# Score matmuls as row tiles of 32 partitions, and the causal mask of the second pass as a selection on GpSimd

## The chip, the cores and the metric

The kernel runs on one core of one Trainium2 chip, in one launch. The metric is the device time of one execution in microseconds. A core has TensorE (matmuls, into PSUM), VectorE, ScalarE, GpSimd and SyncE (DMA issue). Each works through its own list in order, and they wait for each other on semaphores.

## The reference

The input is x of 4 batches x 1024 tokens x 128 channels. Two blocks follow; each is a residual around layer normalisations.

```python
# block 1: causal attention with ALiBi, 16 heads of 8 channels
scores = einsum('bhqd,bhkd->bhqk', q, k) * 8 ** -0.5 + slope[h] * (i - j)
scores = where(tril, scores, -inf)
x = x + layernorm(softmax(scores) @ v @ Wo + bo)
# block 2, on layernorm(x): attention without a mask, then a mixture of 8 experts
y = y + layernorm(attention(y)); y = y + layernorm(moe(y))
out = x + layernorm(y)
```

Both attentions run over all 1024 tokens with 16 heads of 8 channels.

## The kernel before

The program is a row pass, a first attention (`at1`, causal, about 48 to 740 us), a second row pass, a second attention (`at2`, no mask, about 803 to 1726 us), and a tail with the experts. Both attentions are the function `attention` with another `Plan`.

Heads are taken in groups of four; a group of one batch is a slot `s`, 16 in all. A head has 32 of the 128 partitions: its 8 channels three times over (high and low parts of a split, for precision in fp32r) and rows for the ALiBi term and the maximum. For each slot there are two passes over the scores:

- pass `a` (line 333): queries on the output partitions, keys along the columns. VectorE takes the maximum of each row (line 466). In the causal plan keys beyond the query tile are left out, and the diagonal block of 128 x 128 gets -1e30 by a second matmul (line 337). Chunks with 128 or 256 keys are packed, four or two heads to one matmul of 512 columns: 38 chunks per slot, 22 of them with a mask. The second attention has 64 of 512 columns.
- pass `b` (line 360): keys on the partitions, queries along the columns, with the negated maximum of the query in the contraction (`fqm`). In the causal plan eight of twelve blocks have a diagonal, masked by another matmul (line 363). ScalarE takes the exponential (line 415) into `probs`. The `pv` step (line 378) multiplies them by the values and by a column of ones: four matmuls per block, each head to its own 32 output partitions (the profile shows eight instructions).

Score matmuls contract over all 128 partitions: the keys are kept in four copies, `km`, each with the rows of the other heads set to zero. `proj` (lines 201 to 203 and 316) projects queries or keys of half a sequence into the bank `misc`. ScalarE copies it to `u` (line 404), and the split follows: `hi`, `part`, then `fq` for queries, or `fk` and the masked write of `km` (2048 elements per partition, line 569) for keys. The first slot's split is VectorE's (lines 442 to 454); all others are GpSimd's (lines 556 to 569), three slots ahead of use.

The order is written out in `Plan.body` and followed by every engine. A slot is a list of steps, one per block (12 causal, 16 otherwise). Step i holds, in this order: the four `b` matmuls of block i+2, interleaved with three to five `a` chunks of the next slot; `m` (the maxima are finished on VectorE, line 474); `proj`; `otr` and `mtr` (four turning matmuls each); `pv` of block i+1; `oev` (PV is copied out). In the causal plan `proj` is at steps 1, 2, 5, 6. The scores have three banks per pass, PV one, and projections and turns share `misc`. The prologue does the projections of slots 0 to 2 and pass `a` of slot 0. The last three slots have no `proj`, and the last one no `a`.

## Time and profile before

| | us |
|---|---|
| median of 3 runs | 2288.22 |
| lowest, highest | 2284.65, 2291.63 |
| span of the profiled execution | 2287.5 |
| TensorE busy | 2102.9 |
| VectorE busy | 1671.8 |
| ScalarE busy | 1373.5 |
| GpSimd busy | 977.3 |

The span runs from the first to the last instruction of the profiled execution. The profile gives no time for that execution beside its span; the median of the runs is 0.7 us longer. Busy time is the union of the instructions of an engine. Ends of matmuls are modelled, so successive matmuls overlap in the timeline; the distance between their starts is what tells the pace. The granted clock (PEclk) is TensorE's as a share of full speed.

### The profile page before, as it was taken

How to read it: one execution, taken by the hardware profiler on the slowest of the kernel's cores; microseconds unless marked ns; L12 is line 12 of the kernel's file. 1: busy time of each engine (PE TensorE's matmuls, PEld its weight loads, DVE VectorE, ACT ScalarE, POOL GpSimd, SP SyncE). 2: the span in 40 equal slices, each digit the busy share in tenths (PEclk: the TensorE clock that was granted, in tenths of full speed). 3: DMA queues.
4: the chain of work that ended last, by engine and by line, in shares of the span. 5: the costliest groups of instructions: out<-in, count | busy, mean ns of one | idle time of the engine just before them, and what ended most of it. 6: DMA issues, size and time to landing. Idle time of an engine off the chain costs nothing. (4 is left out here: it accounts for less than half of the span.)

```text
span 2287.5 us, 41083 instructions
## 1 busy us (share of the span) xinstructions
PE 2102.9 (92%) x11100; PEld 1223.1 (53%) x11100; DVE 1671.8 (73%) x3157; ACT 1373.5 (60%) x2647; POOL 977.3 (43%) x744
## 2 busy tenths in 40 slices
PE   5899999999999679999999999999993999999996
PEld 4455555555554534555555555555531666666664
DVE  5766667666672787777777777778822899998986
ACT  4266566666666616666666666666672655555654
POOL 3665464553610355333333333342002466565554
PEclk7799999999999679999999999999996999999998
DMA  2000000000000300000000000000001100000000
GB/s 59 1 2 1 3 1 1 2 2 1 1 1 2 110 0 1 2 1 1 2 1 1 2 1 1 1 1 1 1 1 61 51 19 19 2 19 19 19 10 10
DMA packets 27508, 24.96 MB, mean 11 GB/s; under 512 B 2409, under 2 KB 21110, under 8 KB 27282
## 3 DMA queue, kind: packets, MB, share of 16 engines
q1 hardware_dynamic: 26400, 21.91, 3.2%
q8 instruction: 103, 1.69, 0.3%
q14 instruction: 123, 1.01, 0.2%
q10 hardware_dynamic: 882, 0.36, 0.1%
HBM read 13.87 MB, written 6.29 MB: 9 GB/s over the span
## 5 line engine op out<-in xcount | busy, mean ns | idle before, releaser
L466 DVE TENSOR_REDUCE at_mx<-at_a 128x1 f32<-128x512 f32 (+3 forms) x1632 | 1010.8, 675 | 358.7 <-PE at_a L333 249.5
L415 ACT ACTIVATE at_probs<-at_b 128x512 f32<-128x512 f32 (+3 forms) x1792 | 888.6, 558 | 474.0 <-PE at_b L360 292.7
L333 PE MATMUL at_a<-at_km,at_fq 128*128 128x512 f32 (+1 forms) x1632 | 704.8, 439 | 20.4 <-DVE at_mx L466 9.8
L360 PE MATMUL at_b<-at_fqm,at_km 128*128 128x512 f32 (+3 forms) x1792 | 710.8, 404 | 11.4 <-ACT at_probs L415 7.6
L333 PEld LDWEIGHTS at_a<-at_km,at_fq 128*128 128x128 f32 x1632 | 316.3, 194 | 290.0 <-DVE at_mx L466 224.4
L360 PEld LDWEIGHTS at_b<-at_fqm,at_km 128*128 128x128 f32 x1792 | 339.8, 191 | 205.5 <-ACT at_probs L415 120.3
L378 PE MATMUL at_pv<-at_probs,at_vst 128*32 128x512 f32 (+3 forms) x3584 | 437.9, 561 | 1.5 <-ACT at_probs L415 1.5
L556 POOL TENSOR_TENSOR at_hi<-at_u,split_sign 128x512 fp32r<-128x512 f32 x120 | 124.9, 1041 | 441.1 <-ACT at_u L404 306.5
L1172 ACT ACTIVATE t_hid<-t_bank_h,b1t 128x512 f32<-128x512 f32 x256 | 174.3, 689 | 195.9 <-DVE t_hid_lo L1306 113.1
L1306 DVE TENSOR_TENSOR t_hid_lo<-t_hid,t_hid_hi 128x512 fp32r<-128x512 f32 x256 | 225.6, 917 | 15.0 <-ACT t_hid_hi L1179 11.8
L569 POOL TENSOR_TENSOR at_km<-at_fk,head_mask 128x2048 fp32r<-128x2048 f32 x60 | 216.1, 3602 | 11.2 <-POOL at_fk L567 11.0
L1340 POOL TENSOR_TENSOR t_hid_hi<-t_hid,pow_cols 128x512 fp32r<-128x512 f32 x112 | 141.1, 1275 | 129.6 <-ACT t_hid L1172 129.0
L404 ACT ACTIVATE at_u<-at_misc,bias 128x512 f32<-128x512 f32 x128 | 88.2, 689 | 124.7 <-PE at_misc L203 58.0
L526 POOL COPY at_vst<-tokens 128x256 f32 (+1 forms) x32 | 13.0, 405 | 328.5 <-PE at_pv L378 328.2
L201 PE MATMUL t_bank_y<-t_hid_hi,t_w2hi 128*128 128x512 f32 x256 | 106.6, 416 | 31.3 <-DVE t_weighed L1315 26.8
L559 POOL TENSOR_TENSOR at_part<-at_hi,split_sign 128x512 f32<-128x512 f32 x120 | 125.0, 1042 | 21.4 <-POOL at_hi L556 21.4
L378 PEld LDWEIGHTS at_pv<-at_probs,at_vst 128*32 128x32 f32 x3584 | 70.6, 108 | 117.1 <-ACT at_probs L415 85.1
L363 PE MATMUL at_b<-ident,causal_mask 128*128 128x128 bf16 x512 | 117.8, 232 | 0.0
L203 PE MATMUL t_bank_y<-t_hid_hi,t_w2lo 128*128 128x512 f32 x256 | 102.2, 399 | 0.0
L202 PE MATMUL t_bank_y<-t_hid_lo,t_w2hi 128*128 128x512 f32 x256 | 101.9, 398 | 0.0
L337 PE MATMUL at_a<-causal_mask,ident 128*128 128x128 bf16 (+2 forms) x352 | 91.7, 260 | 0.0
L564 POOL TENSOR_TENSOR at_fq<-at_part,at_u 128x512 fp32r<-128x512 f32 x60 | 77.0, 1284 | 10.7 <-POOL at_part L559 10.7
(211 smaller groups left out, 2410.3 us busy)
## 6 DMA issues: line engine op xcount, KB each, us to landing
t_raw<-L_ffn_W SPq DMA_DIRECT2D x16, 256.0 KB, 3.1
x_first<-L_attn_x SPq DMA_DIRECT2D x4, 512.0 KB, 7.3
second_x_in<-L_attn_x SPq DMA_DIRECT2D x8, 256.0 KB, 3.1
kept<-second_joined SPq DMA_DIRECT2D x8, 256.0 KB, 2.6
kept_u<-second_normed SPq DMA_DIRECT2D x8, 256.0 KB, 2.0
t_heads_in<-tokens SPq DMA_DIRECT2D x8, 256.0 KB, 2.6
t_u_in<-kept_u SPq DMA_DIRECT2D x8, 256.0 KB, 3.1
t_x_in<-kept SPq DMA_DIRECT2D x8, 256.0 KB, 3.1
```

Of the source, the lines that this page charges most:

```text
L333: mm = pe.matmul(scores, fq[g][:, qt * P:(qt + 1) * P], km[g][:, heads[0]:heads[0] + k, kh * HALF:kh * HALF + w], start=True, stop=not dia ...
L360: mm = pe.matmul(out[:, 0:w], km[g][:, j, kt * P:(kt + 1) * P], fqm[g % 2][:, q0:q0 + w], start=True, stop=not diagonal)
L363: mm = pe.matmul(out[:, 0:P], causal_mask[:, :], ident16[:, :], start=False, stop=True)
L378: mm = pe.matmul(pv_bank[HW * j:HW * (j + 1), HALF - w:HALF], vst[g % 2][:, kt, j, :], probs[(n % 2) * GH + j][:, 0:w], start=(kt == 0), s ...
L415: act.activation(probs[(t % 2) * GH + j][:, 0:w], b_bank[n % 3][:, 0:w], ACT.Exp).then_inc(exp_done, 1)
L466: dve.tensor_reduce(mx[:, kh, qt, heads[0]:heads[0] + k], a_bank[n % 3][:, 0:k * w].rearrange("p (k w) -> p k w", k=k), AX.X, ALU.max).the ...
L556: pool.tensor_tensor(hi[:, :], un[:, :], split_sign[:, 2:3].broadcast_to([P, HALF]), ALU.add).then_inc(pool_step, 1)
L559: pool.tensor_tensor(part[:, :], hi[:, :].bitcast(F32), split_sign[:, m:m + 1].broadcast_to([P, HALF]), ALU.mult).then_inc(pool_step, 1)
L569: pool.tensor_tensor(km[g][:, :, half], fk[:, None, :].broadcast_to([P, GH, HALF]), head_mask[:, :, None].broadcast_to([P, GH, HALF]), ALU ...
L1172: act.activation(hid[:, f, :], h_bank[f][:, :], ACT.Gelu, bias=b1t[:, f, e:e + 1]).then_inc(hidden["act"], 1)
L1306: dve.tensor_tensor(hid_lo[e % 2][:, f, :], hid[:, f, :], hid_hi[e % 2][:, f, :].bitcast(F32), ALU.subtract).then_inc(hidden["dve"], 1)
L1340: pool.tensor_tensor(out, a, b, op).then_inc(stage["pool"], 1)
```

## The change

- `km` goes. Score matmuls of both passes take the 32 partitions of one head from `fk` and `fq` or `fqm`, so that they are row tiles of 32 x 128. GpSimd and VectorE no longer write the masked copies; a key split ends with `fk`.
- Each chunk of pass `a` has one head. The causal plan now has 48 chunks per slot, 32 with a mask, and the mask matmul stays a full 128 x 128. `a_next`, the share of the next slot's chunks in the last four steps, becomes 16 of 48.
- The heads of a block of pass `b` are taken in the order 2, 3, 0, 1 (`b_head`).
- Pass `b` has no mask matmul. The exponentials of a block lie together in one `probs` tile, and for the eight diagonal blocks GpSimd runs an `affine_select` over 4 x 128 elements per partition that puts zero where the key is later than the query. `pv` of such a block waits for it (`masked`). GpSimd meets it in its list where `pv` stands.

```diff
-                per = max(1, HALF // n)
-                per = 4 if per >= 4 else per
-                for j in range(0, GH, per):
-                    self.chunks.append((qt, kh, list(range(j, j + per)), n))
+                for j in range(GH):
+                    self.chunks.append((qt, kh, j, n))
...
+        self.diagonals = [t for t, (qh, kt) in enumerate(self.quads) if causal and kt * P >= qh * HALF]
...
+def b_head(n):
+    return (n + 2) % GH
...
-        km = [sb(f"km{i}", [P, GH, T], F32R) for i in range(4)]
+        fk = [sb(f"fk{i}", [P, T], F32R) for i in range(4)]
...
-        probs = [sb(f"probs{i}", [P, HALF]) for i in range(8)]
+        probs = [sb(f"probs{i}", [P, GH, HALF]) for i in range(2)]
...
-                        mm = pe.matmul(scores, fq[g][:, qt * P:(qt + 1) * P],
-                                       km[g][:, heads[0]:heads[0] + k, kh * HALF:kh * HALF + w],
+                        rows = slice(HW * j, HW * (j + 1))
+                        mm = pe.matmul(scores, fq[g][rows, qt * P:(qt + 1) * P],
+                                       fk[g][rows, kh * HALF:kh * HALF + w],
                                        start=True, stop=not diagonal)
                         if diagonal:
-                            mm = pe.matmul(scores[:, :, w - P:w], ident16[:, :],
-                                           causal_mask[:, None, :].broadcast_to([P, k, P]),
+                            mm = pe.matmul(scores[:, w - P:w], ident16[:, :], causal_mask[:, :],
                                            start=False, stop=True)
...
-                        mm = pe.matmul(out[:, 0:w], km[g][:, j, kt * P:(kt + 1) * P],
-                                       fqm[g % 2][:, q0:q0 + w], start=True, stop=not diagonal)
-                        if diagonal:
-                            mm = pe.matmul(out[:, 0:P], causal_mask[:, :], ident16[:, :],
-                                           start=False, stop=True)
+                        rows = slice(HW * j, HW * (j + 1))
+                        mm = pe.matmul(out[:, 0:w], fk[g][rows, kt * P:(kt + 1) * P],
+                                       fqm[g % 2][rows, q0:q0 + w], start=True, stop=True)
...
                         done(pe, exp_done, NB, s, GH * n + GH - 1)
+                        if n in plan.diagonals:
+                            done(pe, masked, len(plan.diagonals), s, plan.diagonals.index(n))
...
                 for what, ds, n in steps:
                     s = s0 + ds
+                    if what == "pv" and n in plan.diagonals:
+                        await_(exp_done, NB, s, GH * n + GH - 1)
+                        block_ = probs[n % 2][:, :, 0:P]
+                        pool.affine_select(block_, block_, [[0, GH], [1, P]], ALU.is_ge, 0.0, base=0,
+                                           channel_multiplier=-1).then_inc(masked, 1)
                     if what != "proj":
                         continue
...
-                    if m == 0:
-                        pool.tensor_tensor(fq[g][:, half], part[:, :], un[:, :],
-                                           ALU.add).then_inc(split_done, 1)
-                    else:
-                        pool.tensor_tensor(fk[:, :], part[:, :], un[:, :], ALU.add).then_inc(pool_step, 1)
-                        await_(pool_step, count, s, step + 2)
-                        pool.tensor_tensor(km[g][:, :, half],
-                                           fk[:, None, :].broadcast_to([P, GH, HALF]),
-                                           head_mask[:, :, None].broadcast_to([P, GH, HALF]),
-                                           ALU.mult).then_inc(split_done, 1)
+                    dst = fk if m else fq
+                    pool.tensor_tensor(dst[g][:, half], part[:, :], un[:, :], ALU.add).then_inc(split_done, 1)
```

## Rows read from the trace of the kernel before

**Rows 1.** The page's first part: busy us (share of the span) xinstructions, whole run.
```profile
PE 2102.9 (92%) x11100; PEld 1223.1 (53%) x11100; DVE 1671.8 (73%) x3157; ACT 1373.5 (60%) x2647; POOL 977.3 (43%) x744
```

**Rows 2.** Windows of the two attentions; columns: length, five engines' busy us, PEclk, DMA.
```profile
120.00:700.00 580.00, 576.14 (x3761) 308.73 (x3760) 390.45 (x684) 363.34 (x764) 272.27 (x194) 0.99 0.01 2
900.00:1600.00 700.00, 693.30 (x3637) 374.54 (x3636) 545.36 (x951) 477.26 (x895) 262.56 (x188) 1.00 0.01 1
```

**Rows 3.** Starts of the step m (line 474), first and second attention.
```profile
L474 DVE TENSOR_TENSOR at_mfull<-at_mx x15: 193/381/669, 137.0 to 705.2; 128x32 f32<-128x32 f32 x15
...
L474 DVE TENSOR_TENSOR at_mfull<-at_mx x15: 191/192/194, 915.4 to 1674.9; 128x32 f32<-128x32 f32 x15
```

**Rows 4.** Waits in the second attention: us in total, times, longest.
```profile
DVE at_mx L466 <- PE at_a L333: 145.9, 195, 3.1
```

**Rows 5.** Timeline of TensorE, second attention: start us, us, then the instruction.
```profile
1209.11 1.07 PE L378 MATMUL at_pv<-at_probs,at_vst 128*32 128x512 f32 x8
...
1211.83 0.40 PE L360 MATMUL at_b<-at_fqm,at_km 128*128 128x512 f32 x1
1212.16 1.06 PE L378 MATMUL at_pv<-at_probs,at_vst 128*32 128x512 f32 x8
1213.16 0.50 PE L333 MATMUL at_a<-at_km,at_fq 128*128 128x512 f32 x1
1213.49 0.39 PE L360 MATMUL at_b<-at_fqm,at_km 128*128 128x512 f32 x1
1213.72 0.40 PE L333 MATMUL at_a<-at_km,at_fq 128*128 128x512 f32 x1
```

**Rows 6.** Timeline, second attention: VectorE in a full step, ScalarE in the last slot.
```profile
892.58 2.48 DVE L466 TENSOR_REDUCE at_mx<-at_a 128x1 f32<-128x512 f32 x4 [0.55 <-PE at_a L333]
...
1714.06 2.07 ACT L415 ACTIVATE at_probs<-at_b 128x512 f32<-128x512 f32 x4 [0.55 <-PE at_b L360]
```

**Rows 7.** Groups of GpSimd by form, first attention: busy us, mean ns, idle before.
```profile
L569 POOL TENSOR_TENSOR at_km<-at_fk,head_mask 128x2048 fp32r<-128x2048 f32 x26 | 93.6, 3602 | 4.6 <-POOL at_fk L567 4.5 <-ACT at_u L404 0.2
L556 POOL TENSOR_TENSOR at_hi<-at_u,split_sign 128x512 fp32r<-128x512 f32 x51 | 53.1, 1041 | 150.1 <-PE at_b L360 124.8 <-ACT at_u L404 20.7 <-POOL at_km L569 4.6
L526 POOL COPY at_vst<-tokens 128x256 f32<-128x256 f32 x3 | 1.2, 400 | 48.4 <-PE at_pv L378 48.4
```

**Rows 8.** Timeline of VectorE in the prologue of the second attention.
```profile
807.81 2.29 DVE L454 TENSOR_TENSOR at_km<-at_fk,head_mask 128x2048 fp32r<-128x2048 f32 x1
```

**Rows 9.** Groups of line 466 by form, first attention.
```profile
L466 DVE TENSOR_REDUCE at_mx<-at_a 128x1 f32<-128x512 f32 x342 | 220.5, 687 | 115.4 <-PE at_a L333 74.2 <-PE at_a L337 40.8
L466 DVE TENSOR_REDUCE at_mx<-at_a 128x1 f32<-128x384 f32 x116 | 64.4, 558 | 42.3 <-PE at_a L337 39.1
```

**Rows 10.** Timeline of TensorE, first attention: two scores around a masking matmul.
```profile
404.44 0.40 PE L333 MATMUL at_a<-at_km,at_fq 128*128 128x512 f32 x1
...
405.03 0.40 PE L333 MATMUL at_a<-at_km,at_fq 128*128 128x512 f32 x1
```

**Rows 11.** Timeline, first attention, a projection step: TensorE, ScalarE, then GpSimd.
```profile
403.53 0.64 PE L378 MATMUL at_pv<-at_probs,at_vst 128*32 128x256 f32 x8
...
403.72 0.69 ACT L404 ACTIVATE at_u<-at_misc,bias 128x512 f32<-128x512 f32 x1 [0.92 <-PE at_misc L316]
...
404.75 1.04 POOL L556 TENSOR_TENSOR at_hi<-at_u,split_sign 128x512 fp32r<-128x512 f32 x1 [9.86 <-PE at_b L360]
...
407.19 1.29 POOL L567 TENSOR_TENSOR at_fk<-at_part,at_u 128x512 f32<-128x512 f32 x1 [0.18 <-POOL at_part L559]
408.66 3.60 POOL L569 TENSOR_TENSOR at_km<-at_fk,head_mask 128x2048 fp32r<-128x2048 f32 x1 [0.18 <-POOL at_fk L567]
```

**Rows 12.** TensorE after an idle stretch: timeline row, then windows (columns as rows 2).
```profile
860.52 0.63 PE L346 MATMUL at_misc<-ident,at_mpad 128*128 128x128 f32 x4 [2.64 <-DVE at_mpad L481]
...
862.00:865.00 3.00, 2.90 (x8) 2.00 (x9) 1.92 (x4) 0.00 (x0) 2.82 (x2) 0.50 0.01 3
865.00:868.00 3.00, 2.71 (x8) 1.14 (x6) 3.00 (x6) 1.01 (x2) 2.72 (x2) 0.93 0.00 0
```

More of the change, by code:

```diff
@@ L261, in attention @@
         o_done = sem("o_done")
+        masked = sem("masked")
         init = sem("init")
@@ L319, in emit @@
                     elif what == "a":
-                        qt, kh, heads, w = plan.chunks[n]
+                        qt, kh, j, w = plan.chunks[n]
                         _, g = where(b0, g0, ds)
@@ L327, in emit @@
                         done(pe, a_read, NA, s - back, k)
[L328 removed]
+                        scores = a_bank[n % 3][:, 0:w]
                         diagonal = causal and kh * HALF + w == (qt + 1) * P
[L331 to L334 removed]
+                        rows = slice(HW * j, HW * (j + 1))
+                        mm = pe.matmul(scores, fq[g][rows, qt * P:(qt + 1) * P],
+                                       fk[g][rows, kh * HALF:kh * HALF + w],
                                        start=True, stop=not diagonal)
                         if diagonal:
[L337 to L338 removed]
+                            mm = pe.matmul(scores[:, w - P:w], ident16[:, :], causal_mask[:, :],
                                            start=False, stop=True)
@@ L357, in emit @@
                         w = (qh + 1) * HALF - q0
-                        diagonal = causal and kt * P >= qh * HALF
                         out = b_bank[n % 3]
-                        mm = pe.matmul(out[:, 0:w], km[g][:, j, kt * P:(kt + 1) * P],
-                                       fqm[g % 2][:, q0:q0 + w], start=True, stop=not diagonal)
-                        if diagonal:
-                            mm = pe.matmul(out[:, 0:P], causal_mask[:, :], ident16[:, :],
-                                           start=False, stop=True)
+                        rows = slice(HW * j, HW * (j + 1))
+                        mm = pe.matmul(out[:, 0:w], fk[g][rows, kt * P:(kt + 1) * P],
+                                       fqm[g % 2][rows, q0:q0 + w], start=True, stop=True)
                         mm.then_inc(b_made, 1)
@@ L438, in emit @@
                         un = u[n % 2]
-                        own = 5 * h if m else 5 * h + 3
+                        own = 4 * h + 2 * (n % 2)
                         done(dve, proj_read, 4, s, n)
@@ L447, in emit @@
                         dve.wait_ge(dve_step, own + 2)
-                        if m == 0:
-                            dve.tensor_tensor(fq[g][:, half], part[:, :], un[:, :],
-                                              ALU.add).then_inc(split_done, 1)
-                        else:
-                            dve.tensor_tensor(fk[:, :], part[:, :], un[:, :], ALU.add).then_inc(dve_step, 1)
-                            dve.wait_ge(dve_step, own + 3)
-                            dve.tensor_tensor(km[g][:, :, half],
-                                              fk[:, None, :].broadcast_to([P, GH, HALF]),
-                                              head_mask[:, :, None].broadcast_to([P, GH, HALF]),
-                                              ALU.mult).then_inc(split_done, 1)
+                        dst = fk if m else fq
+                        dve.tensor_tensor(dst[g][:, half], part[:, :], un[:, :], ALU.add).then_inc(split_done, 1)
                     elif what == "a":
-                        qt, kh, heads, w = plan.chunks[n]
+                        qt, kh, j, w = plan.chunks[n]
                         done(dve, a_made, NA, s, n)
@@ L464, in emit @@
                             done(dve, m_step, 2, s - 1, 0)
[L465 to L467 removed]
+                        dve.tensor_reduce(mx[:, kh, qt, j:j + 1], a_bank[n % 3][:, 0:w],
                                           AX.X, ALU.max).then_inc(a_read, 1)
@@ L504, in _ @@
         def _(pool):
-            for semaphore, per in ((split_done, 4), (v_staged, 1)):
-                pool.sem_inc(semaphore, per)
+            for semaphore, per in ((split_done, 4), (v_staged, 1), (masked, len(plan.diagonals))):
+                if per:
+                    pool.sem_inc(semaphore, per)
             pool.memset(mpad[:, :, :], 0.0).then_inc(init, 1)
@@ L552, in emit @@
                     await_(split_done, 4, s, n - 1)
-                    step = 5 * h if m else 5 * h + 3
+                    step = 4 * h + 2 * (n % 2)
                     half = slice(h * HALF, (h + 1) * HALF)
```

26 lines of the change are left out of this document (7 added, 19 removed).

## The prediction

> **What bounds the kernel now.** I read the busy shares of the page first [rows 1]: TensorE 92%, VectorE 73%, ScalarE 60%, GpSimd 43%. Shares average over stages, so next the windows of the two attention stages [rows 2]. In both TensorE is busy 99% of the time; VectorE is busy 67% of the first (causal) attention and 78% of the second. The step `m` runs once per slot (a slot is one batch and group of four heads), so its first and last start give the period [rows 3]: (705.2 - 137.0)/14 = 40.6 us causal, (1674.9 - 915.4)/14 = 54.25 us non-causal. The waits agree: in the second attention VectorE waited 145.9 us for score matmuls [rows 4]. The timeline shows how full TensorE is: a score matmul of 512 columns starts 0.23 us after the last one, a PV group takes 1.00 us until the next matmul starts, and one step of eight scores and PV takes 3.05 us [rows 5]. The chain of waits covers little of these stages; I use it for nothing.
>
> **Step 1: scores as row tiles.** 96 to 128 score matmuls per slot contract over 32 rows instead of 128. They could only become cheaper by running beside each other: the order a j, b j+2, a j+1, b j+3 puts neighbours on different partitions and banks. No row shows a row tile. The nearest is PV: eight instructions of 512 columns, in four column tiles, take 1.00 us together while a single score takes 0.23 [rows 5]; column tiles do overlap. Bounds for one row-tiled score: 0.23 us (no overlap) and 0.06 (four at once). I take 0.12, their geometric mean, since PV shows overlap in the other direction of the array only.
> The Trainium skill ("TensorE: Matmul & The Clock Gate", Part 3) gives four row tiles of 512 columns a speedup of 3.07; by that the score would be 0.076 us. No run here shows it so far.
>
> Second attention: a step on TensorE becomes 8 x 0.12 + 1.00 + 0.2 = 2.2 us, under VectorE's 2.48 us for four reductions [rows 6]. So VectorE is late next. It is busy 0.779 x 54.25 = 42.3 us per slot; three banks cover 3 x 0.6 = 1.8 us of TensorE being elsewhere, enough for a PV (1.3 us with its changes), not for PV plus projection (2.0) or plus turns (1.85) with 0.4 us until the first score is out. Eight such places lose about 0.55 us each: 46.8 us. Gain 7.45 x 15 = 112 us. The last slot has no reductions; its steps go from ScalarE's 2.07 busy + 0.55 waiting [rows 6] towards 2.2: 5 us. Together **-117** (bounds: 0 without overlap, -176 if VectorE never starves, 11.3 x 15 + 7).
>
> **Step 2: no head-masked key copies.** The masked write of 2048 elements goes from GpSimd (3.60 us, two per slot) and, in each prologue, two of 2.29 us from VectorE [rows 7, 8]. In the loop GpSimd's split is three slots ahead: hidden, worth nothing by itself. In the prologues the first scores wait for VectorE's splits, so about 3 us each: **-6** (0 to -10).
>
> **Step 3: causal chunks one head at a time.** 48 reductions for 38: six packed ones of 512 become eight of 128 and eight of 256. From 687 ns at 512 and 558 at 384 [rows 9] a 128 costs about 0.30 and a 256 about 0.43: 5.8 - 4.1 = +1.7 us, VectorE 27.3 + 1.7 = 29.0 us, still under TensorE. The masking matmuls of the first pass go from 22 to 32 per slot.
>
> **Step 4: masks on TensorE.** A masking matmul today lengthens the stream by 0.12 us: two scores and a mask take 405.03 - 404.44 = 0.59 against 2 x 0.23 [rows 10]. The second pass loses 32 of them, 4 us of 40.6. The first pass keeps its own, now a 128-row matmul between 32-row ones. The trace shows what a change of array shape costs: before each PV the next start comes 0.33 us after a 512-column matmul in place of 0.23 [rows 5], 0.10 more, and the same on the way back. So one masked score with the b score beside it: 0.1 + 0.05 + 0.1 + 0.08 of exposed load + 0.17 of columns = 0.5 us, 32 times = 16. The 32 scores left over: 3.8. Unchanged: PV 11.8 (six groups of 1.00, two each of 0.79, 0.57 and 0.36 by their columns, and 12 x 0.2 for changes [rows 5, 11]), projections 3.6 (14 matmuls of 512 columns at 0.23 to 0.33), turns 2.1 (four sets at 0.63 less 0.1 of overlap [rows 12]). Sum 37.3. The same working for the kernel before gives 8.4 + 3.0 of masks for pass a, 8.6 + 4.0 for pass b, and these 17.5: 41.5 where 40.6 is measured, so I take 36.5 (bounds 32, mask as cheap as today, and 41).
> The rule that speaks against this change is in the skill ("TensorEngine Tiling (Array Packing)", Key Properties): changing the tiling mode drains the engine. The 0.10 us in the rows agrees in kind. By a full drain (0.39 us, the duration of a 512 score) each masked pair would be 0.3 us longer, and the causal slot 9 us longer.
>
> **Step 5: the selection on GpSimd.** This is the step that decides. The selection is issued at `pv` in program order; in the list of a step `proj` stands before `pv`, and GpSimd is in order. TensorE now waits at a diagonal `pv` for `masked`, and everything of the next step is queued behind it. Causal projections are at steps 1, 2, 5, 6, the diagonal PVs at steps 0-2 (blocks 1-3) and 7-11. At steps 1 and 2 the selection is thus behind the split of a projection that TensorE has just made. The links are in [rows 11]: PV could start at 403.53; ScalarE's copy ends at 404.41; the three splitting operations start at 404.75 and end at 408.48; the selection can start at 408.66, where the masked copy does now. With 1.04 us for it and 0.2 for the hand-over PV starts at 409.9: a stall of 6.3 us. At step 2 the projection has no ALiBi matmul, and the same links give 6.3 again. At step 7 TensorE passes PV 7 (1.2 us) and the scores of step 7 (2.1) first: 3 us left. Elsewhere the exponentials are done a step earlier (about 2 us before) and the selection is hidden; if it took over 2 us it would bind there too.
> Duration of the selection, 512 elements per partition: no row has it. Below: a copy of 256 takes 0.40, so 0.8; above: 3.60, the masked write [rows 7]. I take 1.04, the elementwise operation of the same size, the nearest row [rows 7]. At 3.6 each stall grows by 2.6, 13 slots x 7.7 = +100.
> Stalls: 6.3 + 6.3 + 3 = 15.6 us, in the 13 slots that project three ahead.
>
> **Step 6: the clock.** After 2.64 us of idle TensorE was granted 0.50 in the next 3 us and 0.93 in the 3 after it [rows 12]: the lower of its two levels, 1.2 GHz, for some 3.4 us. Three stalls per slot cost up to 1.7 us of warm work each; part hides behind VectorE: 4 us (bounds 0 and 6).
>
> Causal slot: 36.5 + 15.6 + 4 = 56.1, +15.5 x 13 = +202. Two other looped slots at 36.5: -8; the last -4. First attention **+190** (bounds: 32 + 15 + 0 = 47 gives +60; 41 + 16 + 6 = 63 gives +290).
>
> **Sum:** +190 - 117 - 6 = +67 us on the profiled execution with its span of 2287.5 us; what lies outside the span I leave as it is. The span is 0.7 us under the median of 2288.22 (runs 2284.65 to 2291.63), so 2355 us for the median.
>
> **Rivals.**
> A, faster: the second attention falls to VectorE's floor (-150 to -176) and the causal slot is cheap between its stalls, 33 + 15 + 1 = 49 us, +8.4 x 13 - 20 = +90. Total 90 - 160 - 6 = -76: 2212 us. For it: VectorE leaves 22% of the second attention idle and TensorE has slack in the new step. Against it: it needs masked pairs at about 0.35 us, cheaper than the two shape changes in the trace allow. With the second attention as forecast the total crosses zero at a stalled slot of 40.6 + 135/13 = 51 us; from there A decides.
> B, no overlap: row tiles run one after another at 0.23 us because each writes all 128 partitions of PSUM. Second attention unchanged, causal slot 41 + 16 + 4 = 61: +265 - 6. Total 2547 us. Against it: PV's column tiles overlap [rows 5].
> C, the stalls are not there (GpSimd is ahead, or the selection overtakes): causal 36.5, -4.1 x 16 = -66; total -189: 2099 us. Against it: the list's order, and the 3.7 us from 404.75 to 408.48 in [rows 11].
>
> **How the numbers follow.** Forecast 0.56; A 0.22; B 0.17; C 0.05. About 0.3% is what a measurement tells from no change. The forecast's own spread (2260 to 2440) leaves a little under 2295, so slower is 0.51 + 0.17 = 0.69; the band within 0.3% gets 0.04 between A and the forecast; faster 0.27. Range: from A's inner half, 2225, up to 2450, which leaves out C, the low end of A, and B.
>
> **What would show it.** Changed profile: score starts about 0.1 us apart and a period near 47 us in the second attention; VectorE over 88% busy there; in the causal one two idle stretches of TensorE of about 6 us per slot, each ending with a selection on GpSimd, and a granted clock under 0.9 on average; a selection near 1.04 us. I am wrong if score starts stay 0.23 us apart (B), if the idle stretches are missing (C), or if masked pairs cost 0.35 us (A).

## The result and the profile after

The changed kernel took 2908.68 us, median of 4 runs (2898.94 to 2924.59), beside 2286.83 us for the kernel before (4 runs, 2284.65 to 2291.63). The ratio is 1.272, 95% interval 1.267 to 1.277: 27% slower. The forecast was 2355 us in a range of 2225 to 2450. The direction was right, the size far outside the range. A run over 1.5% above the fastest of its kernel is marked slow; without such runs e17's median is 2457.64 us and e19's 2242.6, in place of the 2462.01 and 2260.68 given below.

The profiled execution has a span of 2922.9 us, 635.4 more than before. The page of the kernel after: busy shares, then TensorE's busy tenths and the granted clock in 40 slices.

```profile
PE 2426.0 (83%) x10908; PEld 1131.0 (39%) x10908; DVE 1693.7 (58%) x3313; ACT 1379.3 (47%) x2647; POOL 835.7 (29%) x812
...
PE   5888887888888888997788888888888849999997
...
PEclk6555555555555555556579989979999759999998
```

TensorE's share fell from 92% [rows 1] to 83%, and its granted clock is at the lower of its two levels (1.2 of 2.4 GHz) through nearly all of the first attention. The starts of `m` in the two attentions of the kernel after answer to [rows 3]:

```profile
L465 DVE TENSOR_TENSOR at_mfull<-at_mx x15: 191/273/714, 193.2 to 1302.7; 128x32 f32<-128x32 f32 x15
...
L465 DVE TENSOR_TENSOR at_mfull<-at_mx x15: 192/193/194, 1536.9 to 2285.9; 128x32 f32<-128x32 f32 x15
```

The causal slot is (1302.7 - 193.2)/14 = 79.25 us (before: 40.59) and the non-causal one 53.5 (before: 54.25). The 15 starts span 1109.5 us in place of 568.2: 541 of the 635 us. A further 56 lie ahead of them (193.2 against 137.0) and 21 between the last causal `m` and the first of the second attention. These three are in the main the first attention with its prologue, +618 us where +190 was forecast. The second attention's sixteen starts of `m` (the first at 1477.2, before at 858.5) take 8 us less than before, and what follows its last `m` 24 us more (637.0 against 612.6): +16 us where -117 was forecast. Windows of the two attentions after (columns as in [rows 2]):

```profile
330.00:530.00 200.00, 168.56 (x630) 66.26 (x628) 72.55 (x145) 65.56 (x133) 45.73 (x51) 0.53 0.00 1
...
1480.00:2280.00 800.00, 678.33 (x4161) 255.21 (x4165) 630.92 (x1096) 542.71 (x1025) 182.47 (x173) 0.94 0.01 1
```

**The predicted waits are there.** TensorE's wait at PV in the first attention after, in us, times and longest:

```profile
PE at_pv L379 <- POOL at_probs L536: 165.1, 40, 5.5
```

And one of them in the timeline (start, us, instruction, idle before): the query split ends, the selection starts at once, and PV starts when it is over. A single selection takes 636 ns (the group of 124 in the first attention).

```profile
519.39 1.27 POOL L561 TENSOR_TENSOR at_fq<-at_part,at_u 128x512 fp32r<-128x512 f32 x1 [0.18 <-POOL at_part L556]
...
520.61 1.23 POOL L536 TENSOR_SCALAR_AFFINE_SELECT at_probs<-at_probs 128x512 f32<-128x512 f32 x2
...
521.30 1.05 PE L379 MATMUL at_pv<-at_probs,at_vst 128*32 128x512 f32 x4 [1.32 <-POOL at_probs L536]
```

**A masked pair, at the full clock and at half.** TensorE in the first attention after:

```profile
504.80 0.49 PE L362 MATMUL at_b<-at_fqm,at_fk 32*128 32x512 f32 x1
504.80 0.44 PE L336 MATMUL at_a<-at_fk,at_fq 32*128 32x384 f32 x1
505.22 0.23 PE L340 MATMUL at_a<-causal_mask,ident 128*128 128x128 bf16 x1
505.38 0.49 PE L362 MATMUL at_b<-at_fqm,at_fk 32*128 32x512 f32 x1
...
540.19 0.68 PE L362 MATMUL at_b<-at_fqm,at_fk 32*128 32x384 f32 x1
540.19 0.79 PE L336 MATMUL at_a<-at_fk,at_fq 32*128 32x512 f32 x1
540.91 0.29 PE L340 MATMUL at_a<-causal_mask,ident 128*128 128x128 bf16 x1
541.13 0.68 PE L362 MATMUL at_b<-at_fqm,at_fk 32*128 32x384 f32 x1
```

The two row tiles start together; then the 128-row mask comes 0.42 us after them, and the next pair 0.16 us after the mask: 0.58 us for the pair (0.94 at half clock). For scale: before, two scores and a mask took 0.59 us one after another [rows 10]. The overlap that the row tiles win is given back at the mask. Full clock is rare in this stage: it holds here for some 4 us.

**The second attention** reaches the overlap but not the gain. TensorE after, from one PV to the next, in a step without projection or turns:

```profile
1802.89 1.06 PE L379 MATMUL at_pv<-at_probs,at_vst 128*32 128x512 f32 x8
1803.89 0.50 PE L336 MATMUL at_a<-at_fk,at_fq 32*128 32x512 f32 x1
1803.89 0.51 PE L362 MATMUL at_b<-at_fqm,at_fk 32*128 32x512 f32 x3
1804.23 0.40 PE L336 MATMUL at_a<-at_fk,at_fq 32*128 32x512 f32 x2
1805.17 0.49 PE L336 MATMUL at_a<-at_fk,at_fq 32*128 32x512 f32 x1 [0.54 <-DVE at_mx L458]
...
1805.68 1.06 PE L379 MATMUL at_pv<-at_probs,at_vst 128*32 128x512 f32 x8
```

One PV to the next takes 2.79 us where it took 3.05 [rows 5]. The fourth `a` score waits for VectorE to read a bank. VectorE in turn still waits for scores, 157.1 us of 800 (before 145.9 of 700 [rows 4]), the same fifth of the time: both engines wait, in turn.

### The profile page after: what moved, and what is told of

It is laid out like the page before. It is cut to its first block and busy times, and to the rows that moved or that the text cites. A ratio compares the mean times of both kernels' runs of the same rounds, so it can differ in the third digit from the quotient of the medians.

```text
span 2922.9 us, 41409 instructions
## 1 busy us (share of the span) xinstructions
PE 2426.0 (83%) x10908; PEld 1131.0 (39%) x10908; DVE 1693.7 (58%) x3313; ACT 1379.3 (47%) x2647; POOL 835.7 (29%) x812
## 3 DMA queue, kind: packets, MB, share of 16 engines
q14 instruction: 127, 1.04, 0.1%
## 5 line engine op out<-in xcount | busy, mean ns | idle before, releaser
L458 DVE TENSOR_REDUCE at_mx<-at_a 128x1 f32<-128x512 f32 (+3 forms) x1792 | 1041.4, 629 | 868.6 <-PE at_a L336 432.2
L336 PE MATMUL at_a<-at_fk,at_fq 32*128 32x512 f32 (+3 forms) x1792 | 763.2, 564 | 134.1 <-DVE at_mx L458 124.7
L362 PE MATMUL at_b<-at_fqm,at_fk 32*128 32x512 f32 (+3 forms) x1792 | 732.2, 574 | 45.4 <-ACT at_probs L416 45.4
L379 PE MATMUL at_pv<-at_probs,at_vst 128*32 128x512 f32 (+3 forms) x3584 | 589.2, 741 | 165.4 <-POOL at_probs L536 165.4
L336 PEld LDWEIGHTS at_a<-at_fk,at_fq 32*128 32x128 f32 x1792 | 339.4, 234 | 626.5 <-DVE at_mx L458 461.8
L362 PEld LDWEIGHTS at_b<-at_fqm,at_fk 32*128 32x128 f32 x1792 | 301.8, 230 | 290.1 <-ACT at_probs L416 128.6
L553 POOL TENSOR_TENSOR at_hi<-at_u,split_sign 128x512 fp32r<-128x512 f32 x120 | 124.6, 1038 | 984.5 <-ACT at_u L405 984.1
L536 POOL TENSOR_SCALAR_AFFINE_SELECT at_probs<-at_probs 128x512 f32<-128x512 f32 x128 | 80.7, 636 | 399.9 <-ACT at_probs L416 399.9
L340 PE MATMUL at_a<-causal_mask,ident 128*128 128x128 bf16 x512 | 143.7, 281 | 0.0
L340 PEld LDWEIGHTS at_a<-causal_mask,ident 128*128 128x128 bf16 x512 | 52.2, 102 | 153.9 <-issue 144.1
L206 PE MATMUL at_misc<-turned_hi,w_hi 128*128 (+1 forms) x128 | 86.8, 678 | 12.9 <-PEq L598 8.2
L483 DVE RECIPROCAL at_rec<-at_misc 128x16 f32<-128x16 f32 x64 | 16.4, 256 | 137.3 <-PE at_misc L386 137.0
```

What stands on the lines that cost most here:

```text
L206: pe.matmul(out, a[0], b[0], start=start, stop=False)
L336: mm = pe.matmul(scores, fq[g][rows, qt * P:(qt + 1) * P], fk[g][rows, kh * HALF:kh * HALF + w], start=True, stop=not diagonal)
L340: mm = pe.matmul(scores[:, w - P:w], ident16[:, :], causal_mask[:, :], start=False, stop=True)
L362: mm = pe.matmul(out[:, 0:w], fk[g][rows, kt * P:(kt + 1) * P], fqm[g % 2][rows, q0:q0 + w], start=True, stop=True)
L379: mm = pe.matmul(pv_bank[HW * j:HW * (j + 1), HALF - w:HALF], vst[g % 2][:, kt, j, :], probs[n % 2][:, j, 0:w], start=(kt == 0), stop=(n = ...
L458: dve.tensor_reduce(mx[:, kh, qt, j:j + 1], a_bank[n % 3][:, 0:w], AX.X, ALU.max).then_inc(a_read, 1)
```

## The experiments

All slots below are (last - first start of `m`)/14, and "clock" is the granted one in windows of the first attention, both of the profiled execution. Totals are medians. The diffs are against the kernel named.

**1. The selection issued early: e1.** Against the kernel after: GpSimd selects at the last exponential of a block, ahead of `proj` in its list.

```diff
-                    if what == "pv" and n in plan.diagonals:
-                        await_(exp_done, NB, s, GH * n + GH - 1)
+                    if what == "b" and n % GH == GH - 1 and n // GH in plan.diagonals:
+                        await_(exp_done, NB, s, n)
```

> The changed kernel, but GpSimd runs each selection where the last exponential of its block stands in the list, ahead of that step's projection split. Stall theory (the idle stretches of TensorE behind GpSimd cause both the waiting and the half clock of the first attention): the two 5.5 us waits per slot go, the granted clock there rises from 0.52 to at least 0.95, the slot falls from 80.5 to about 38 us, total near 2250 us. Tile theory (a stream of row tiles broken by full-array masks does not get the full clock back once it is lost, and the loop and the prologue lose it without any stall): only the waits go, 12.7 us per projecting slot and the clock stays near 0.52: slot about 67 us, total about 2740 us.

Measured: 2664.95 us, ratio 1.163 (1.157 to 1.170). Slot 61.85. No wait of TensorE for a selection is left, and TensorE is 97% busy, but the clock stays low. Window of e1:

```profile
330.00:530.00 200.00, 194.00 (x796) 79.16 (x796) 90.44 (x182) 82.71 (x170) 58.76 (x65) 0.59 0.01 1
```

The waits and what hangs on them are worth 17.4 us of a slot, of which the waits themselves were 12.7; 21 us over the slot before remain without them. Neither theory's clock or total came out (0.95 and 2250, 0.52 and 2740), but the clock that stays low without a wait is the tile theory's.

**2. No masks in pass `a`, selection late: e2.** Against after (the maximum may then cover later keys, which changes no softmax):

```diff
-                        diagonal = causal and kh * HALF + w == (qt + 1) * P
+                        diagonal = False
```

> The changed kernel without the mask matmuls of pass a (32 per causal slot), the selections stay late. The row maximum is then taken over up to 127 later keys as well, which only shifts the exponent. Stall theory: the waits stay, so the clock stays near 0.52; only 32 masks at about 0.4 us go: slot about 68 us, total about 2720 us. Tile theory: with the shape changes between the scores gone the clock comes back between stalls, as it mostly does in the second attention: clock 0.7 or more, slot under 58 us, total under 2560 us.

Measured: 2667.5 us, ratio 1.164 (1.151 to 1.178), slot 63.36, clock 0.52. TensorE waited 169.2 us for selections, as in the kernel after: the masks and the waits are separate costs. The tile theory's clock without the masks, 0.7 or more, did not come. The same edit on e1 is e5:

> The changed kernel with the early selection and without the mask matmuls of pass a: row tiles alone, neither waits for GpSimd nor full-array masks between the scores. If the masks between row tiles are what holds the clock down, the first attention now behaves like the second: clock 0.85 or more, slot about 37 us, total about 2250 us. If row tiles of themselves do not regain it, the clock there stays under 0.65 and the slot is about 52 us, total about 2480 us.

Measured: 2456.98 us, ratio 1.073 (1.068 to 1.077), slot 50.31, clock 0.59 to 0.61. From e2 to e5 the slot lost 13.05 us, and e2's waits are 169.2/13 = 13.0 per slot: here the waits cost just themselves. From e1 to e5 it lost 11.5 for 32 masks. With neither masks nor waits the clock is still 0.6.

**3. The late selection on full arrays: e3.** The kernel before, with the change's selection and without its row tiles.

```diff
-                        mm = pe.matmul(out[:, 0:w], km[g][:, j, kt * P:(kt + 1) * P],
-                                       fqm[g % 2][:, q0:q0 + w], start=True, stop=not diagonal)
-                        if diagonal: ...
+                        mm = pe.matmul(out[:, 0:w], km[g][:, j, kt * P:(kt + 1) * P],
+                                       fqm[g % 2][:, q0:q0 + w], start=True, stop=True)
...
+                    if what == "pv" and n in plan.diagonals: ...  # GpSimd: affine_select
```

> The kernel before with one part of the change alone: the second pass masked by the late selection on GpSimd, scores still full-array with masked key copies. Waits per slot are longer than in the changed kernel, because the split of a key still has its masked copy: about 9.5 + 5.9 + 5 us. Stall theory: with such idle stretches the clock is near 0.55 in the first attention, slot above 80 us, total above 2850 us. Tile theory: full-array scores get the clock back within about 3.4 us, clock near 0.8, slot 58 to 62 us, total 2520 to 2590 us.

Measured: 2613.45 us, ratio 1.141 (1.135 to 1.146), slot 61.43: the tile theory's slot and clock, its total missed by 23 us. Waits and a window of e3:

```profile
PE at_pv L379 <- POOL at_probs L546: 276.7, 39, 9.3
```

```profile
330.00:530.00 200.00, 132.65 (x715) 70.43 (x715) 85.30 (x145) 76.92 (x163) 78.34 (x71) 0.81 0.00 1
```

Here the selection also stands behind the masked key copy, so the waits are longer (21 us per slot) than in the kernel after. Yet the clock is 0.81 with TensorE busy 66% of the time. With row tiles it is 0.53 at 84%. Waits alone don't hold the clock at half.

e3 also tells what waits cost full arrays in clock, as an estimate: 61.43 less 21.3 of waits leaves 40.1 us, and the slot before without its 32 masks of pass `b` (0.12 us each by [rows 10]) is 36.7. The difference is 3.4 us.

**4. Row tiles with every mask on TensorE: e4.** Against after: no selection at all, pass `b` masked by 128-row matmuls.

```diff
+                        if t in plan.diagonals:
+                            mm = pe.matmul(out[:, 0:P], causal_mask[:, :], ident16[:, :],
+                                           start=False, stop=True)
```

> The changed kernel with the row tiles alone: pass b is masked by a matmul on TensorE as before, there is no selection and no wait for it. Stall theory: no idle stretches, clock 0.95 or more, slot about 42 us, total about 2310 us. Tile theory: the clock stays near 0.5 although TensorE never waits for GpSimd, slot about 75 us, total about 2830 us.

Measured: 2989.33 us, ratio 1.305 (1.301 to 1.309), slot 83.04: slower than the kernel after and than the tile theory's 2830 us, and without a wait for GpSimd. Window of e4:

```profile
530.00:730.00 200.00, 198.62 (x681) 84.75 (x681) 70.09 (x138) 61.37 (x126) 27.94 (x27) 0.53 0.00 1
```

TensorE is 99% busy at half clock. This run decides between waits and stream: the stream alone does it. It also shows the clock falling with no gap at all. One slot of e4 around its stretch at full clock:

```profile
589.00:602.00 13.00, 13.00 (x39) 4.45 (x39) 3.90 (x6) 4.71 (x8) 4.38 (x4) 0.50 0.01 2
602.00:605.50 3.50, 3.50 (x14) 1.69 (x13) 1.67 (x3) 1.47 (x3) 2.30 (x2) 0.99 0.00 0
605.50:637.00 31.50, 31.50 (x105) 14.40 (x104) 10.08 (x23) 7.61 (x17) 0.40 (x1) 0.50 0.00 1
```

TensorE is busy in all of it, as the profile counts busy. Just before the rise it ran three projection matmuls and a PV, all over 128 rows (598.09 to 601.5); until the fall it ran scores as row tiles, each with its mask. Between 190 and 1350 us e4 has 18 such rises. In the 5 us before each TensorE ran three projection matmuls or four turns, and then a PV; not every such group is followed by one. All but one of the stretches last 3 to 4 us, and TensorE has no idle time in the 6 us before any of the 18 falls.

**5. The masks as row tiles too: e15 and e16.** e15 is e1 with pass `a`'s masking matmul over the 32 partitions of its head (it then applies a part of the mask only, and the maximum may cover later keys); e16 does so in both passes, on e4 (one edit shown).

```diff
-                            mm = pe.matmul(scores[:, w - P:w], ident16[:, :], causal_mask[:, :],
+                            mm = pe.matmul(scores[:, w - P:w], ident16[rows, :], causal_mask[rows, :],
```

> The kernel of the early selection (causal slot 61.9 us, clock about 0.60) with the 32 mask matmuls of pass a kept in number and columns, but taken over the 32 partitions of their head, the shape of the scores beside them (the mask then reaches only those 32 queries; the others' maximum covers later keys too). If changes of array shape cost the time and hold the clock down, the slot falls to about 50 us, as without the masks. If it is the extra small matmuls that cost, it stays at 59 us or more.

Measured: 2502.19 us, ratio 1.092 (1.089 to 1.096), slot 50.78 where e1 has 61.85: as many masks of as many columns, 0.35 us less for each. The clock didn't rise:

```profile
330.00:530.00 200.00, 189.36 (x927) 81.51 (x927) 100.19 (x212) 90.86 (x198) 72.12 (x79) 0.53 0.00 1
```

It is 0.53 to 0.57 up to 730 us, e1's 0.59 to 0.61. So the 11.1 us are the change of shape and the overlap that it breaks, and no gain of clock; against e5, without any mask, row-tiled masks cost 0.5 us a slot.

> Row tiles in both passes, no selection, and every masking matmul (32 of pass a, 32 of pass b per slot) contracts over the 32 partitions of its head, so only a part of the mask is applied; nothing but PV, projections and turns changes the shape of the array, and no wait for GpSimd is left. The same kernel with 128-row masks took 2989.33 us: slot 83.04, granted clock 0.52 while TensorE was 99% busy. Theory M (the changes between 32-row and 128-row matmuls hold the clock down): granted clock in the first attention above 0.8, slot 42 to 46 us, total 2310 to 2380. Rival R (a causal stream of row tiles does not regain the clock even so): clock 0.5 to 0.65, slot 55 to 65, total 2520 to 2680.

Measured: 2432.52 us, ratio 1.063 (1.060 to 1.066), slot 47.26 where e4 has 83.04. Window of e16:

```profile
330.00:530.00 200.00, 184.62 (x1225) 87.32 (x1223) 115.40 (x246) 104.81 (x231) 58.91 (x56) 0.73 0.01 2
```

64 matmuls in another shape cost 35.8 us, 0.56 each, part of it clock (0.52 to 0.55 in e4, 0.64 to 0.73 in e16). The slot and the total are between what theory M and theory R gave.

**6. Nothing but row tiles: e17.** Against e4: no mask in either pass.

> Row tiles in both passes and no mask in any form (the causal mask is left out in both passes; the blocks beyond the diagonal are still skipped): the score matmuls alone. Theory M: no mask, no shape change, no wait, so the clock is full: slot about 34 to 37 us (VectorE 29, ScalarE under it), total 2200 to 2250. Rival R: the clock stays at 0.5 to 0.65 and the slot is 45 to 50 us, total 2370 to 2450; the run with an early selection and no pass-a mask had 50.31.

Measured: 2462.01 us, ratio 1.069 (1.060 to 1.079), slot 49.61. Window of e17, and the longest of TensorE's waits there:

```profile
330.00:530.00 200.00, 183.07 (x890) 72.94 (x888) 108.39 (x232) 97.25 (x216) 55.17 (x52) 0.61 0.01 1
```

```profile
PE at_a L335 <- DVE at_mx L459: 38.1, 102, 0.9
```

This holds for R, whose slot and clock came (its total, up to 2450, was a little short): with no mask, no shape change but PV's, projections' and turns', and no wait over 0.9 us, a causal stream of row tiles gets 0.59 to 0.61 of the clock where full arrays got 0.99 [rows 2]. It does less work than e16, and its profiled slot is 2.35 us longer at a lower clock; the totals of the two don't differ beyond their intervals.

**7. One head per chunk on full arrays: e18.** Against before:

```diff
-                for j in range(0, GH, per):
-                    self.chunks.append((qt, kh, list(range(j, j + per)), n))
+                for j in range(GH):
+                    self.chunks.append((qt, kh, [j], n))
```

> The kernel before with one change: each pass-a chunk has one head (48 chunks per causal slot, 32 with a mask, in place of 38 and 22), still full-array matmuls on masked keys. Theory: the columns are the same and ten more masks of 0.12 us and ten more instructions cost 1.2 to 2 us per slot; slot 42 to 42.6, total 2305 to 2320, clock unchanged at 0.96 over the run. Rival: short single-head chunks with their masks are themselves what lets the clock fall in the first attention: clock there under 0.9, slot over 45, total over 2360.

Measured: 2310.36 us, ratio 1.008 (1.006 to 1.010), slot (726.8 - 143.5)/14 = 41.66, clock of the run 0.958. Window of e18:

```profile
330.00:530.00 200.00, 198.24 (x1345) 112.25 (x1346) 134.44 (x275) 122.73 (x256) 105.05 (x74) 1.00 0.01 2
```

The smaller chunks cost 1.1 us a slot and no clock. e4 differs from e18 in the row tiles and what goes with them (no masked key copies, the order of heads in pass `b`), so it is the row tiles; the order of heads was tried in the second attention only (e20).

**8. A full-array matmul to lift the clock: e10.** Against e1, one more matmul over 128 rows per block, overwritten by the score behind it.

```diff
+                        if n % GH == 0:
+                            pe.matmul(out[:, 0:w], fk[g][:, kt * P:(kt + 1) * P],
+                                      fqm[g % 2][:, q0:q0 + w], start=True, stop=True)
```

> The kernel of the early selection with work added: ahead of the first score of each block of pass b one full-array matmul of the same columns into the same bank, whose result is overwritten (12 or 16 per slot, 0.1 to 0.23 us each at full clock). Tile theory: this raises the granted clock of the first attention well above 0.60, so that adding work makes the kernel faster than the 2665 us without it. If the clock has another cause, it stays at 0.60 and the added matmuls cost about 12 x 0.3 x 16 = 58 us in the first attention and 40 in the second: total about 2760 us.

Measured: 3045.37 us, ratio 1.330 (1.318 to 1.341); slots 67.01 (e1: 61.85) and, in the second attention, (2443.6 - 1375.8)/14 = 76.27 (e1: 53.49). A window of e10 there, its lowest of five between 1300 and 2300:

```profile
1500.00:1700.00 200.00, 186.10 (x680) 62.22 (x675) 98.79 (x167) 84.12 (x159) 32.26 (x31) 0.60 0.00 1
```

My expectation failed, the rival's 2760 too. In the first attention the clock stayed (0.61 to 0.65 up to 730 us, e1's 0.59 to 0.61). In the second, one matmul of another shape per block took it to between 0.60 and 0.88 in those five windows, where e1 has 0.92 to 0.97 between 1300 and 1900.

**9. Row tiles in the second attention alone: e6 and e20.** The first attention is before's. e20 takes pass `b`'s heads in the order 0, 1, 2, 3 (`return n % GH`), so that neighbours share their 32 rows.

> The first attention as in the kernel before, row tiles in the second attention only (it has no masks and no selection). The second attention of the changed kernel took about 905 us against 921 before, with its clock at 0.5 in the prologue and after loop turns: total 2265 to 2280 us, about 1% faster at most. If the second attention suffered only from the state in which the first one left the clock, it would be faster here: slots of 52 us throughout and a total near 2240 us.

> Row tiles in the second attention alone, with the heads of pass b taken in the order 0, 1, 2, 3, so that an a score and the b score behind it use the same 32 rows. With the order 2, 3, 0, 1 the same kernel took 2318.66 us, slot 55.07. Theory O (row tiles overlap only on different rows): neighbours now run in pairs one after another, scores start 0.12 to 0.23 us apart instead of four within 0.01, TensorE is back at 95% busy or more, slot 56 to 60, total 2335 to 2400. Rival V (VectorE's banks set the pace, not the overlap): nothing changes, 2318 within 8 us.

Measured: e6 2318.66 us, ratio 1.012 (1.010 to 1.015), slot 54.7; e20 2352.46 us, ratio 1.031 (1.025 to 1.037), slot 56.1. The second attention of the change, alone, is no gain but a loss of 1.2%, worse than either expectation (2280, 2240). e20's total is in theory O's range, though TensorE is 86% busy where O had 95. In e20 scores start 0.33 us apart in place of together, for 1.4 us a slot (the clock over the run is 0.902): of these row tiles only those on different rows overlapped. Little hangs on it; TensorE waited for VectorE to read a bank in this order too.

**10. PV inside the step, and the full-array variants: e7, e12, e9.** e7 is before with the early selection and no pass `a` masks; e12 has its projections at steps 0, 1, 3, 5; e9 is e12 with row tiles in the second attention and PV ahead of the last two entries of a step.

```diff
-        self.proj_steps = [free[len(free) * i // 4] for i in range(4)]
+        self.proj_steps = [0, 1, 3, 5] if causal else [free[len(free) * i // 4] for i in range(4)]  # e12
...
-            out += self.interleave(bs, ass)
+            both = self.interleave(bs, ass)
+            out += both[:-2] + values + both[-2:]  # e9: values is the step's pv and oev
```

> Full-array scores with masked key copies as before; in the first attention pass b is masked by the selection on GpSimd, issued early (ahead of the split), and the mask matmuls of pass a are left out (the row maximum then also covers up to 127 later keys, which leaves the softmax as it is). Tile theory: clock stays at 0.97 or more, TensorE loses 32 + 22 masks of 0.12 us and more per slot, slot from 40.6 to about 34 us, total about 2185 us. Stall theory would have selections behind masked key copies (3.6 us) hold TensorE at one place per slot: slot 37 to 40 us and a clock near 0.8, total 2240 to 2280 us.

> The full-array kernel with the early selection and no masks in pass a, with the four projections of a causal slot at steps 0, 1, 3, 5 instead of 1, 2, 5, 6, so that GpSimd has finished the masked key copy before the selection of block 8 is due. In the run without this TensorE waited 49 us for selections in all (17 waits) and lost the clock after each. If that is where the gain of the removed masks went: no wait left, clock 0.97 or more in the first attention, slot from 40.1 to about 36 us, total 2215 to 2235 us. If the masks were hidden work, the slot stays at 40 us and the total at 2285 us.

> The same first attention, and row tiles in the second one with the PV group issued ahead of the last two scores of a step, where TensorE otherwise waits for VectorE to free a bank. In the changed kernel TensorE idled about 0.5 us per step there and VectorE about 0.3 us per step after PV. If that order is what kept the row tiles from paying, a warm slot falls from 52 to about 46 us, and the total is 80 to 130 us under the run with full-array scores in both. If the granted clock decides, it falls below 0.9 with the fuller stream not helping, and the slot is 54 us or more: no gain or a loss.

Measured: e7 2288.15 (0.999, 0.998 to 1.000), e12 2294.51 (1.002, 1.000 to 1.003), e9 2285.8 us (0.997, 0.995 to 0.9997). In e7 TensorE still waits for selections behind GpSimd's masked key copies:

```profile
PE at_pv L379 <- POOL at_probs L546: 42.6, 15, 3.2
```

This run missed both expectations (2185, and 2240 to 2280), and e12, expected at 2215 to 2235 without waits, has more of them (58.2 us in 25): the move only shifts them. e9's slot in the second attention is 53.0 where e12 has 54.15, and its total 9 us less: far from the 80 to 130 us that I had expected if the order of PV were what held the row tiles back.

**11. The better version: e13, and e19 on top.** e13 is the kernel before without pass `a`'s masks (the edit of e2; pass `b` keeps its own on TensorE). e19 adds e9's second attention.

> The kernel before with one edit: the 22 mask matmuls per causal slot of pass a left out (the row maximum also covers up to 127 later keys, which leaves the softmax as it is). Each lengthens the stream by 0.12 us and more: 22 x 0.13 = 2.9 us of 40.6 per slot, 15 to 16 slots, total about 2243 us. If they were hidden: 2287 us.

> The first attention as in the kernel before without the pass-a masks (the maximum may then cover keys beyond the diagonal; the softmax is the same), and the second attention with row tiles and PV ahead of the last two entries of a step. Theory: the two changes are in separate stages and add up. The first took 33 us off a run; the second's slot was 53.14 where full-array ones take 54.2 to 54.5, so 16 to 20 us more: 2235 to 2245 us, clock of the first attention 0.99 or so and of the second 0.9. Rival: the row-tiled second attention loses the clock for a stretch at random and gives the gain back: slot 55, 2265 us.

Measured: e13 2258.31 us, ratio 0.985 (0.983 to 0.987), slot (674.8 - 139.8)/14 = 38.21. Window of e13's first attention:

```profile
130.00:680.00 550.00, 542.98 (x3486) 294.84 (x3484) 385.72 (x687) 358.00 (x770) 265.46 (x191) 0.99 0.01 2
```

22 masks less at 0.12 us are 2.6 us; the slot lost 2.4. e13 beats both kernels, by less than the 2243 us that I had expected. e19: 2260.68 us (2233.27 to 2275.48), ratio 0.989 (0.984 to 0.995). The profiled one is its fastest, with a slot of 51.3 us in the second attention. Its runs lie 42 us apart, those of the kernel before beside them 11: with row tiles the clock over the run goes from 0.89 to 0.92 between executions. That spread belongs to the kernel, so no gain over e13 is shown.

## Why the prediction was right or wrong

**Direction right, range wrong. The step that failed is Step 6, the clock, with Step 4's masked pair beside it.** The forecast causal slot was 36.5 (work) + 15.6 (stalls) + 4 (clock) = 56.1; 79.25 was measured. The stalls came out at 165.1/13 = 12.7. What is left, 66.5 us, stands where I had 40.5. Seen against the 15.5 us that I forecast the slot to lose, it lost 38.7.

**Step 6.** I read the clock's price from [rows 12]: full-array work after an idle stretch, back at the full clock within 6 us. For full arrays the term of 4 us was about right: the estimate from e3, whose waits are longer, is 3.4. I took this recovery for a property of the engine. It is not one of a stream of row tiles. Windows of the second attention after, around a turn of the loop:

```profile
1926.00:1930.00 4.00, 1.32 (x14) 0.71 (x6) 0.82 (x4) 0.00 (x0) 0.00 (x0) 1.00 0.06 14
1930.00:1934.00 4.00, 3.84 (x20) 1.07 (x17) 2.52 (x5) 2.17 (x5) 0.00 (x0) 0.64 0.01 2
...
1950.00:1954.00 4.00, 3.65 (x20) 0.89 (x16) 2.48 (x4) 2.14 (x4) 2.31 (x2) 0.50 0.00 0
...
1978.00:1982.00 4.00, 3.46 (x24) 0.72 (x16) 2.20 (x4) 2.66 (x5) 2.70 (x3) 0.89 0.00 0
```

One gap, and TensorE runs at 0.50 for some 45 us while busy over 90% of the time. In the first attention the clock seldom comes back, and not for long: e4 without a wait (0.53 at 99% busy), e17 without mask or wait (0.61), against e3 with longer waits on full arrays (0.81) and e18 with one-head chunks (1.00 up to 730 us).

That row tiles are the cause is shown by these, for the causal stage; the second attention's stream, with neither masks nor short scores, had 0.94, and its clock came back each time. And it is more than a slow recovery, since e4 falls to 0.50 with TensorE busy throughout. Why stays open: e4's rises follow projections or turns and a PV over 128 rows, but e10 refuted my guess that a full-array matmul now and then would bring the clock.

With my 36.5 us of work, which no run measures, and 2.6 more for 32 masked pairs at 0.58, the clock's term is by difference 79.25 - 12.7 - 39.1 = 27 us, not 4; taking 0.53 of the 66.5 us as the work gives 31. These are estimates. By the first, it is 320 of the 554 us by which the median missed.

The Trainium skill bears on this ("TensorE: Matmul & The Clock Gate", Part 1): idleness halves the clock and busy work restores it. The trace agrees with the first half (the fall after a gap of 2.68 us at 1926.6). The second half fails in e4 at 99% busy, as the profile counts busy, and e4 also falls without idleness.

**Step 4.** The pair at full clock is 0.58 us, not 0.50, with 0.42 from score to mask. I had weighed the drain rule of the Trainium skill ("TensorEngine Tiling (Array Packing)", Key Properties) at 9 us a slot and set it aside for the 0.10 us of [rows 5]. That row was PV behind a full-array score; here the mask starts 0.42 us after row tiles that last 0.44 and 0.49. The trace agrees with the rule in kind. In size, at the full clock 0.58 is nearer to my 0.50 than to the 0.80 that I had worked out from the rule; the 11.1 us a slot between e1 and e15 are at 0.53 to 0.61 of the clock and hold the lost overlap too.

**Step 5** held in place and mechanism: the splits stand ahead of the selection, PV waits, 12.7 us a slot against 15.6. The selection took 0.64 us where I took 1.04. e1 confirms it: moving the issue took all of it away, and 17.4 us of slot. The waits are a third of the 38.7 us that the slot lost and were to be all of it.

**Step 1.** The overlap was right, better than forecast (four scores start together and the next 0.34 us later, 0.085 each; I had 0.12). The gain was not: 46.8 us forecast, 53.5 measured. The step's length is not TensorE's sum but a cycle over both engines: VectorE must free the bank for the fourth score, and no score is made while PV (1.00 us) runs, so it idles again. A step at full clock is 2.79 us where I had 2.48 from VectorE alone, and the two slots that contain a long loss of clock take 63.2 and 71.5 us, the others about 52 (47 without projections). In the last slot, without reductions, I forecast 5 us less; there the clock fell (0.62 over the 44 us behind the last `m`, 0.50 in the next 40), and the time behind the last `m` grew by 24 us.

**Steps 2 and 3.** Step 3's +1.7 us on VectorE is right in kind (a reduction of 128 takes 292 ns, of 256 424, I had 300 and 430), and e18 gives 1.1 us of slot. Step 2's 6 us can't be seen: the prologues run at the low clock too (0.50 from 54 to 106 us), and the first `m` comes at 106.2 in place of 89.8.

**The rivals.** B (2547) was nearest in time and wrong in mechanism: the tiles do overlap. (The 0.51 + 0.17 of the chances is 0.68, not 0.69.) Rival A's second attention at VectorE's floor did not come. I had no rival in which the clock stays low; its bound of 6 us came from one kind of work, and the range with it.

## What to carry to other kernels

In these kernels a row tile beside another was cheap only inside a run of the same shape: before mixing 32-row matmuls with 128-row ones, count the changes, and price each as the wait for the matmul before it to end (0.42 us at full clock here; 0.35 to 0.56 us per mask in all, at the low clock). Look at the granted clock first when a stream of small tiles is slow while its engine is 99% busy, and don't carry a recovery time from full-array rows over to row tiles. An operation on another engine that the next matmul waits for belongs in that engine's list where its input is ready, not where its output is used; and ask first whether it is needed at all (pass `a`'s masks were not; leaving them out gave 1.5%).

## What was not expected of the hardware

- Row-tiled causal scores got 0.52 to 0.61 of the clock at 92 to 99% busy (e4, e17), full arrays 0.81 at 66% busy (e3).
- In e4 the clock fell from 1.00 to 0.50 at 605.5 us, while TensorE was never idle in the 48 us around it; 17 other falls there are alike.
- Less work wasn't faster: e17 has 64 matmuls per slot fewer than e16, and its profiled slot is longer (49.61 against 47.26 us), at a lower clock (0.59 to 0.61 against 0.64 to 0.73).
- One full-array matmul per block of row tiles raised the second attention's slot from 53.5 to 76.3 us (e1, e10).
- `affine_select` of 512 elements per partition takes 636 ns on GpSimd, less than the 1038 of an elementwise operation of the same size.
